# Router logits and small reorderings in a cross-attention and expert kernel on one core

## The reference

```
kv   = ctx @ W_k.T + b_k                       # (4, 512, 128)
out  = layernorm(x) @ kv                       # einsum bij,bjd->bid
sim  = (out @ kv.T) * 512**-0.5
attn = softmax((sim - mean) * rsqrt(var + 1e-6) * gamma + beta)
x    = x + attn                                # (4, 512, 512)
xn   = layernorm(x)
w    = router_weights(xn @ Wr)                 # sigmoid zone, else top 2; (.., 8)
gate, up = xn @ Wg[e], xn @ Wu[e]              # experts 0, 1 add xn @ Ga @ Gb, xn @ Ua @ Ub
y    = sum_e w[e] * ((silu(gate) * up) @ Wd[e] (+ low rank for e < 2))
x    = x + y
```

## Time and profile before

| | us |
|---|---|
| median of three runs | 1042.78 (1042.32 to 1043.09) |
| profiled execution | 1042.92 |
| its span | 1041.2 |
| PE busy | 1027.5 (99%) |
| DVE busy | 754.1 (72%) |
| ACT busy | 460.8 (44%) |
| POOL busy | 83.8 (8%) |

### The profile page before, as it was taken

How to read it: one execution, slowest core, us unless ns; L and a number is a source line. 1 busy time by engine, 2 the same in 40 slices (tenths; PEclk the granted TensorE clock), 3 DMA queues, 4 the chain that set the end, 5 groups by cost and what they waited for, 6 DMA issues and landing times.

```text
span 1041.2 us, 12605 instructions
## 1 busy us (share of the span) xinstructions
PE 1027.5 (99%) x4653; PEld 844.7 (81%) x4653; DVE 754.1 (72%) x1272; ACT 460.8 (44%) x714; POOL 83.8 (8%) x115
## 2 busy tenths in 40 slices
PE   8999999999999999999999999999999999999998
PEld 5887787878888888888888778888888888888887
DVE  7888678977484865758576695886868586977664
ACT  4664463563353353435334344453635263534530
POOL 2611121101001000000100011000000000000000
PEclk9999999999999999999999999999999999999999
DMA  9410104248567483855748674525343544444342
GB/s 303 155 51 1 82 21 162 78 123 284 201 200 265 151 263 132 287 199 193 268 132 287 200 254 122 182 98 218 119 177 100 209 131 166 158 162 162 108 176 81
DMA packets 95709, 173.43 MB, mean 167 GB/s; under 512 B 5728, under 2 KB 62240, under 8 KB 94752
## 3 DMA queue, kind: packets, MB, share of 16 engines
q1 hardware_dynamic: 87584, 125.37, 36.4%
q0 software_dynamic: 7776, 47.19, 12.3%
q10 hardware_dynamic: 288, 0.07, 0.0%
HBM read 111.23 MB, written 61.37 MB: 166 GB/s over the span
## 4 chain that ended last, share of the span: by engine, by line
PE 85%; DVE 7%; ACT 2%; issue 2%; DMA 2%; POOL 0%; SPq 0%; DVEq 0%; ACTq 0%; POOLq 0%
PE gate_up L2083 15%; PE gate_up L2085 15%; PE gate_up L2084 15%; PE tiles L1960 6%; PE tiles L1962 6%; PE tiles L1961 6%; PE tiles L2103 4%; PE tiles L2101 4%; PE tiles L2102 4%; PE gate_up L2040 2%; PE gate_up L2041 2%; PE gate_up L2046 2%; DVE piece_lo L1449 1%; DMA piece<-merged 1%; DVE mids_lo L1531 1%
## 5 line engine op out<-in xcount | busy, mean ns | idle before, releaser
L2083 PE MATMUL gate_up<-xT_hi,piece_hi 128*128 128x512 f32 x448 | 174.9, 391 | 0.6 <-DVE mids L1490 0.3
L2085 PE MATMUL gate_up<-xT_lo,piece_hi 128*128 128x512 f32 x448 | 174.4, 389 | 0.0
L2084 PE MATMUL gate_up<-xT_hi,piece_lo 128*128 128x512 f32 x448 | 174.3, 389 | 0.0
L2083 PE MATMUL gate_up<-tx_hi,piece_hi 128*128 128x512 f32 x336 | 131.0, 390 | 1.1 <-DVE gates L1478 1.1
L2085 PE MATMUL gate_up<-tx_lo,piece_hi 128*128 128x512 f32 x336 | 130.8, 389 | 0.0
L2084 PE MATMUL gate_up<-tx_hi,piece_lo 128*128 128x512 f32 x336 | 130.7, 389 | 0.0
L1449 DVE TENSOR_TENSOR piece_lo<-piece,piece_hi 128x1024 fp32r<-128x1024 f32 x88 | 93.1, 1100 | 28.9 <-ACT piece_hi L977 28.3
L990 ACT ACTIVATE gate_up<-gate_up 128x512 f32<-128x512 f32 x56 | 32.6, 582 | 182.6 <-PE gate_up L2085 121.7
L1960 PE MATMUL tiles<-wd_hi,mids_hi 128*128 128x512 f32 x256 | 99.7, 390 | 0.5 <-DVE mids_lo L1531 0.5
L2083 PEld LDWEIGHTS gate_up<-xT_hi,piece_hi 128*128 128x128 f32 x448 | 84.1, 188 | 19.5 <-issue 0.7
L1962 PE MATMUL tiles<-wd_hi,mids_lo 128*128 128x512 f32 x256 | 99.6, 389 | 0.0
(11 more groups left out here) (226 smaller groups left out, 1925.3 us busy)
## 6 DMA issues: line engine op xcount, KB each, us to landing
piece_spill<-piece_hi POOLq DMA_DIRECT2D x24, 896.0 KB, 4.3
piece_spill<-piece_lo POOLq DMA_DIRECT2D x24, 896.0 KB, 6.8
piece_hi<-piece_spill SPq DMA_DIRECT2D x24, 896.0 KB, 4.5
piece_lo<-piece_spill SPq DMA_DIRECT2D x24, 896.0 KB, 6.5
piece<-in_wg_dram SPq DMA_DIRECT2D x24, 256.0 KB, 4.3
piece<-in_wu_dram SPq DMA_DIRECT2D x24, 256.0 KB, 6.2
merged<-lora_w SPq DMA_DIRECT2D x6, 1024.0 KB, 6.1
wd_raw<-in_wd_dram SPq DMA_DIRECT2D x5, 1024.0 KB, 5.3
```

The costliest lines, as they stand in the source:

```text
L2083: nc.tensor.matmul(dst, w_h, x_h, start=first and kt == 0, stop=False, skip_group_check=True)
L2084: nc.tensor.matmul(dst, w_l, x_h, start=False, stop=False, skip_group_check=True)
L2085: ins = nc.tensor.matmul(dst, w_h, x_l, start=False, stop=last and kt == 1, skip_group_check=True)
```

## The change

It moves work within the queues and adds, at most, semaphore waits; the arithmetic stays.

First half block: units 1 to 3 of the first 256 tokens go through a new function, which runs high × high and high × low first (low part of x) and the low parts of the weights last, and so waits for `w_hi_made` at the start and for the low parts only at the end.

Blocks 0 and 1 (`more`): TensorE transposes the router logits behind `x_times_kv`, into bank 3 of `tiles`; unit 1 waits only for `logitsT_read` (DVE's copy out of bank 2), and `down(n, 0)` waits for `logits_read`. DVE reads the logits behind `add_attention` (in block 0 behind `ln2_stats`), not between the scores. ScalarE has the router functions behind `copy_outT`, in front of `scores_high_parts`. In block 0 the first normalised tile comes between silu 3 and its high part.

Steps of the second stage: a few DVE and ScalarE items change places, in steps 0, 6 and 7.

```diff
--- before.py
+++ after.py
@@ ScalarE, first_expert @@
                 unit(n, 0, tokens)
-                router_functions(n)
+                if not more:
+                    router_functions(n)
                 unit(n, 1, tokens)
...
                 if more:
                     copy_outT(n + 2, tiles)
-                if more:
+                    router_functions(n)
                     scores_high_parts(n + 2)
                 unit(n, 2, tokens)
-                unit(n, 3, tokens)
-                for t in range(TT):
+                if tokens == SECOND:
+                    unit_silu(n, 3, tokens)
+                    normalise(n + 1, 0, more, n + 3)
+                    unit_high_part(n, 3, tokens)
+                else:
+                    unit(n, 3, tokens)
+                    normalise(n + 1, 0, more, n + 3)
+                for t in range(1, TT):
                     normalise(n + 1, t, more, n + 3)
@@ ScalarE, step k @@
                 if k == 0:
+                    copy_p5(j + 3)
                     piece_high_part(j + 4)
-                mid_high_part(k, 0, C22)
-                copy_p5(j + 3)
+                    mid_high_part(k, 0, C22)
+                else:
+                    mid_high_part(k, 0, C22)
+                    copy_p5(j + 3)
@@ DVE, first_expert @@
-                sim_scores(a, logits_of=n)
+                sim_scores(a, logits_of=None if more else n)
...
                 if tokens == SECOND:
                     ln2_stats(a)
+                if more:
+                    read_logits(n, tiles)
+                if tokens == SECOND:
                     unit(n, 2, tokens)
@@ DVE, step 7, step 0, step 6, step 0 @@
+                    mid_low_part(k - 1, 1, C21)
                     t_low_part(6, tx_lo[:, 2, :], x_back[:, 3, :], tx_hi[:, 2, :])
-                    mid_low_part(k - 1, 1, C21)
...
-                    wd_low_part(k)
                     combine(k, GATE, 1, C22)
                     piece_sums(j + 3)
+                    wd_low_part(k)
...
-                    piece_low_part(j + 3)
-                    combine(k, GATE, 1, C22)
                     if k == SWAP - 1:
+                        combine(k, GATE, 1, C22)
+                        piece_low_part(j + 3)
                         back_sum(1, 3, 6)
+                    else:
+                        piece_low_part(j + 3)
+                        combine(k, GATE, 1, C22)
...
                 make_mid(k, 0, C22)
+                if k == 0:
+                    make_mid(k, 0, C21)
                 mid_low_part(k, 0, C11)
...
-                make_mid(k, 0, C21)
+                if k != 0:
+                    make_mid(k, 0, C21)
@@ TensorE, the first half block @@
+            def first_half_unit(f):
+
+                pe.wait_ge(mid_made, FIRST_HALF * FT + f - 1 + EARLIER + UNIT_CREDIT)
+                pe.wait_ge(w_hi_made, f + 1)
...
+                for m in range(2):
+                    dst = gate_up[:, 2 * p + m, FIRST]
+                    for k in range(KT):
+                        nc.tensor.matmul(dst, w_hi[:, m, k, cols], x_hi[:, k, FIRST], start=(k == 0), stop=False)
+                        nc.tensor.matmul(dst, w_hi[:, m, k, cols], x_lo[:, k, FIRST], start=False, stop=False)
+                if f < 3:
+                    pe.wait_ge(w_gu_ready, f + 1)
+                if f >= 2:
+                    pe.wait_ge(w_rest_ready, f - 1)
+                for m in range(2):
+                    for k in range(KT):
+                        ins = nc.tensor.matmul(gate_up[:, 2 * p + m, FIRST], w_lo[:, m, k, cols], x_hi[:, k, FIRST],
+                                               start=False, stop=(k == KT - 1))
+                ins.then_inc(gu_mm, 1)
@@ TensorE, first_expert @@
-                logits(n, gate_up)
-                pe.wait_ge(logits_read, n + 1)
+                if not more:
+                    logits(n, gate_up)
+                    pe.wait_ge(logits_read, n + 1)
+                pe.wait_ge(logitsT_read, n + 1)
                 unit(n, n, 1, tokens)
                 unit(n, n, 2, tokens)
...
                         x_times_kv(a + 1, h, tiles)
+                    logits(n, tiles)
                     pe.wait_ge(kvT_ready, a + 2)
                 unit(n, n, 3, tokens)
                 if more:
                     pe.wait_ge(outT_ready, 2 * a + 4)
+                    pe.wait_ge(logits_read, n + 1)
```

More of the change, by code:

```diff
@@ L52 @@
 SIM_BANK = [2, 3, 0, 1]
+LOGITS_BANK = 3
 STEPS = 2 * (POSITIONS - 1)
@@ L809, in unit, with unit_silu @@
             def unit(n, f, tokens=WHOLE):
+                unit_silu(n, f, tokens)
+                unit_high_part(n, f, tokens)
+            def unit_silu(n, f, tokens):
                 u = n * FT + f + EARLIER
@@ L814, in unit, with unit_high_part @@
                   .then_inc(silu_made, 1)
-                act.wait_ge(mid_made, u + 1 + UNIT_CREDIT)
+            def unit_high_part(n, f, tokens):
+                act.wait_ge(mid_made, n * FT + f + EARLIER + 1 + UNIT_CREDIT)
                 if tokens == WHOLE:
@@ L1341, in read_logits @@
                 dve.wait_ge(logits_mm, a + 1)
-                nc.vector.tensor_reduce(z[:, :, :], banks[:, 3, 0:TT * 2 * E].rearrange("p (t h e) -> p t e h", t=TT, h=2),
+                nc.vector.tensor_reduce(z[:, :, :], banks[:, LOGITS_BANK, 0:TT * 2 * E].rearrange("p (t h e) -> p t e h", t=TT, h=2),
                                         AX.X, ALU.add).then_inc(logits_read, 1)
@@ L1830, in _ @@
                     combine(k, GATE, 1, C12)
-                    piece_low_part(j + 3)
-                    combine(k, GATE, 1, C22)
                     if k == SWAP - 1:
+                        combine(k, GATE, 1, C22)
+                        piece_low_part(j + 3)
                         back_sum(1, 3, 6)
+                    else:
+                        piece_low_part(j + 3)
+                        combine(k, GATE, 1, C22)
+                    if k == SWAP - 1:
                         dve.wait_ge(sums_made, 7)
@@ L2024, in logits @@
                 for t in range(TT):
-                    ins = nc.tensor.transpose(banks[:, 3, t * 2 * E:(t + 1) * 2 * E], logitsT_of(a)[:, t * P:(t + 1) * P],
+                    ins = nc.tensor.transpose(banks[:, LOGITS_BANK, t * 2 * E:(t + 1) * 2 * E], logitsT_of(a)[:, t * P:(t + 1) * P],
                                               small_ident[:, :])
                 ins.then_inc(logits_mm, 1)
+            def first_half_unit(f):
+                pe.wait_ge(mid_made, FIRST_HALF * FT + f - 1 + EARLIER + UNIT_CREDIT)
+                pe.wait_ge(w_hi_made, f + 1)
+                p = f % 2
+                cols = slice(f * P, (f + 1) * P)
+                x_hi, x_lo = block_of(xT_hi, 0), block_of(xT_lo, 0)
+                for m in range(2):
[12 more added lines that the diff above has]
+                ins.then_inc(gu_mm, 1)
             def unit(n, b, f, tokens=WHOLE, tiles_made=None):
@@ L2248, in _ @@
             pe.wait_ge(kvT_ready, 2)
-            for f in range(FT):
-                if f < 3:
-                    pe.wait_ge(w_gu_ready, f + 1)
-                if f >= 2:
-                    pe.wait_ge(w_rest_ready, f - 1)
+            pe.wait_ge(w_gu_ready, 1)
+            unit(FIRST_HALF, 0, 0, FIRST, 2)
+            for f in range(1, FT):
                 if f == FT - 1:
@@ L2257, in _ @@
                         transpose_x2(0, t, tiles[:, SIM_BANK[t], :])
-                unit(FIRST_HALF, 0, f, FIRST, 2 if f == 0 else None)
+                first_half_unit(f)
             def first_expert(n, more, tokens=WHOLE):
```

## The result

The changed kernel takes 1044.2 us (median of 20 executions, 1042.64 to 1044.81), the kernel before 1042.69 (20 executions, 1042.22 to 1043.56). The ratio is 1.0012, 95% interval 1.0006 to 1.0017: slower by 0.12%, under the 0.2% that count as no change here, but beyond its interval. Forecast were 1042.7 and a sum of -0.1. The time lies in my range (1040.9 to 1045.3) and above the range of my likeliest case (1041.7 to 1043.9).

The account below looks back on a forecast made before the run. TensorE, busy 1027.5 of 1041.2 us, was taken as the bound, so only its pauses could change. Terms 0 + 2.5 - 0.1 - 0.4 - 1.36 - 0.73 = -0.1 on the 1042.78 median gave 1042.7 us, range 1040.9 to 1045.3.

Parts of the forecast that it names:

- likeliest case: Whole kernel: the likeliest case by itself was a time of 1041.7 to 1043.9 us.
- First half block, 0: First half block: waits for w_lo go, but unit 3 still hangs on ScalarE's normalised tiles; gain 0, at most 1.3 us.
- Block 0, +2.5: Block 0: DVE's late logits read stalls ScalarE before tanh, so normalised tiles and `down` 2 come 2.5 us later.
- The 3.6 us lie under the later wait and add nothing.: Block 0: TensorE's own 3.6 us pause before `down` is hidden by the later wait for normalised tiles, costing 0.
- The third rival: Block 0: TensorE's clock falls behind the pause, all 24 `down` matmuls run slow, 4.1 us more, 1046.8; chance 0.10.
- Block 1, -0.1: Block 1: TensorE gets 1.0 us ahead, but ScalarE reaches kvT_hi about when it did before; gain 0.1 us.
- Step 0, -0.4: Strassen step 0: pauses for p_sb and mids go, but TensorE then waits for DVE's combinations; gain 0.4 us.
- The moved `wd_low_part`, costed at 0: Strassen step 0: the moved `wd_low_part` falls into idle time in front of `lora_a_low_part`, worth 0.
- Step 6, -1.36: Strassen step 6: TensorE's wait at 580.10 for combination C22, behind a low part, goes entirely; gain 1.36 us.
- step 7, -0.73: Strassen step 7: TensorE's wait near 617 for the last mids_lo, behind two tx_lo, goes entirely; gain 0.73 us.
- the second rival: At 240, 580 and 617: DVE's next wait replaces each one removed, so late gains are lost, 1045.2; chance 0.10.
- The first rival: Block 0: TensorE's order decides, the stall is off the path and the 2.5 us falls away, 1040.2; chance 0.15.

Follow-up runs that it names:

- with the pause filled and the tiles early: DVE's logits read ahead of the statistics, TensorE's pause put back by an added wait and filled with 13 unread matmuls, against the kernel before: 1041.71 us, ratio 0.9989.
- the first blocks alone: The kernel before with all of the change except the reorderings in steps 0, 6 and 7: 1047.06 us, ratio 1.0039.
- the late edits: Run alone: the kernel before with only the reorderings in Strassen steps 0, 6 and 7: 1040.3 us, ratio 0.9978.
- the profile with the unread matmuls in: The changed kernel with 13 matmuls that nobody reads added in TensorE's pause before `down` of block 0, against the kernel before: 1043.19 us, ratio 1.0003.
- ScalarE's router functions later: The changed kernel with ScalarE's router functions of blocks 0 and 1 moved behind silu 2 and its high part, against the kernel before: 1044.13 us, ratio 1.0009.

## Why the prediction was right in its parts and wrong in its sum

- *First half block, 0:* right; alone 1.0000, in the profile -0.03.
- *Block 0, +2.5:* the chain was right to 0.2. Less the 0.96 of the late start, tanh comes at 65.57 (forecast 65.4), silu 2 at 68.89 (68.9), silu 3 at 70.08 (70.0), the tiles end at 73.57 (73.6). Without the fallen clock the block costs +2.57. It costs +2.99, and `down` 2 starts at 74.48 (75.44 less 0.96), where 74.0 was forecast.
- **The step that failed** is this one: "The 3.6 us lie under the later wait and add nothing." The pause (3.34 us shown) was predicted and its cover was counted, but only for the idle time. For that it holds: with the pause filled and the tiles early, TensorE's own delay puts `down` 2 at +1.27 (47.23 less 45.96), less than the +2.57 of the tiles. But behind the pause the clock fell. The 24 matmuls of `down` took 7.17 us (66.60 to 73.77) instead of the 5.57 that they take with the pause filled (65.73 to 71.30), 1.6 more. That is more than the cover: at full clock TensorE's own work would have let `down` 2 start at 73.84, and the tiles allow 75.0, so the cover is 1.15. That is +0.4 in the profiled execution. With the long kind of slow stretch it is +1.4, in the profile of the first blocks alone (49.90 against 48.53).
- *The third rival* had the mechanism and its point of decision ("more than 3 us of work run slow"), but neither its price nor its chance. I took all 24 matmuls as slow, 4.1 us. In the profiles 6 to 13 are slow, and a part of that lay under the late tiles. And I gave it a tenth, because no trace had such a pause; in 29 of the 31 executions of the changed kernel the mean clock is 0.998 or less. (0.999 also occurs with the pause filled, and is no sign of a slow stretch.) The granted clock falls to 0.50 in or behind a pause of 3.3 us in all five profiles that have one. It is 1.00 up to the last matmul in the profiles with the pause filled or avoided. I had set a rule of the Trainium skill beside this rival ("TensorE: Matmul & The Clock Gate", the section "Why this matters for your kernels"): a long enough idle gap between bursts puts TensorE back to its lower clock. The five profiles agree with it, though not every execution seems to: of 57 executions of the four kernels with the unfilled pause, five have a mean clock of 0.999 or 1.0.
- *Block 1, -0.1:* -0.07. *Step 0, -0.4:* -0.29, and as foreseen two short waits are left (0.3 us lost ahead of 242.15 and 0.3 ahead of 243.95), since DVE does the same work in total. The moved `wd_low_part`, costed at 0, is worth about 0.7 (one profile, that of the first blocks alone).
- *Step 6, -1.36, and step 7, -0.73:* -1.39 and -0.74. Nothing was given back behind them; the second rival is out. Alone, with step 0, the late edits bring 2.4 us.
- *The first rival* (the stall in block 0 isn't on the path) is out: with the pause filled, TensorE waits for the normalised tiles, and late tiles cost 1.3 to 1.5 us more than early ones. Moving the one read is worth 4.3 us, but that takes TensorE's pause away as well.

The sum without the clock is +0.3 in the profile with the unread matmuls in and +0.5 by the medians, where -0.1 was forecast; the parts above account for the +0.3 by a tenth or two here and there, and the last 0.2 is within the intervals. The clock adds the rest, 0.3 in the profile and 0.7 to 1.0 by the medians: 1.2 to 1.5 in all. So what the late edits earn (2.4 us by the medians) is more than lost by one read in block 0 that stands three us too late in DVE's order; moving it is worth 4.3.

## What to carry to other kernels

When a pause is called hidden, count what follows it too. Here 3.3 us of idle TensorE brought 3.4 to 6.8 us at 1.2 GHz, which made 24 matmuls take 1.6 us more in the shorter case, and the cover must hold both the idle time and that. A pause that can't be avoided can be filled with matmuls that nobody reads, as a test of what the clock costs or as a stopgap. The better cure is in the order of the engine that is waited for.

A tiny instruction (here 0.2 us, a read of 32 columns) that two engines wait for belongs ahead of the long ones in its queue. Before moving a step earlier, walk through every queue on the way: DVE's, ScalarE's and also POOL's.

## What the runs showed of the hardware

- The slow stretch that goes with the same pause is not always equally long: added up over the windows' granted clock it is 3.4 us in three profiles and 6.8 in two; in both of these and in one of the short ones it begins inside the pause. 6, 8, 8, 12 and 13 matmuls fall into it, by where it lies. And 2 of 11 executions of one of these kernels (ScalarE's router functions later) kept a mean clock of 1.0. The times of that kernel spread from 1041.92 to 1044.48; with the pause filled they lie between 1041.79 and 1042.93.
- A slow matmul of 512 columns starts 0.43 behind the one ahead of it and lasts 0.63, against 0.23 and 0.39.
- The first unit's start varies by 1.3 us (25.15 to 26.49) between profiles. For the latest of them the reason is shown: the temperature's 0.5 KB landed after 8.2 us in the changed kernel's first profile and after 6.0 before. That much of a difference between two profiles of kernels like these says nothing on the change.
